# Audio tower on one core: TensorE's first four slots written out, and a norm on ScalarE

## The reference

```
p   = patches of 16 samples, stride 8                  # 64 x 32 tokens x 1024
h   = relu(p @ W1 + b1) @ W2 + b2                      # 64 x 32 tokens x 256
h  += attention(h)       # 16 heads, "bit-linear": input normalised, quantised to 127 steps,
                         # ternary weights wq, wk, wv; softmax; again normalised, quantised, wo
h  += gate * (norm(h) @ w_expert + b)                  # top-1 of 8, capacity 100 per expert
h  += real part of a decayed linear recurrence over norm(h)
h  += sum over the top 2 of 8 experts: (silu(n @ M1) * (n @ M2)) @ M3,  n = norm(h)
```

## Time and profile before

| | us |
|---|---|
| median of 3 runs | 538.47 (538.28 to 539.43) |
| profiled execution, its own time | 540.12 |
| profiled execution, span from the first to the last instruction | 538.1 |
| TensorE busy (matrix products) | 433.2, 81% |
| VectorE busy | 303.9, 56% |
| ScalarE busy | 199.4, 37% |
| GpSimd busy | 162.2, 30% |
| granted TensorE clock, mean | 0.91 of 2.4 GHz |

### The profile page before, as it was taken

One profiled execution on the slowest core, in us unless ns is written; L12 is line 12 of the kernel. 1 busy time (PEld: TensorE's weight loads), 2 busy tenths in 40 slices (PEclk: granted clock), 3 DMA queues, 4 the chain that ended last, 5 costly groups with the idle time before them and its releaser, 6 DMA issues.

```text
span 538.1 us, 9170 instructions
## 1 busy us (share of the span) xinstructions
PE 433.2 (81%) x3291; PEld 282.7 (53%) x3292; DVE 303.9 (56%) x869; ACT 199.4 (37%) x369; POOL 162.2 (30%) x140
## 2 busy tenths in 40 slices
PE   0698798888657754737759999999799999999991
PEld 0254455555554543536525766676565666566561
DVE  0596958784699899998897577726431111111110
ACT  0244545254357513113422662254323233223321
POOL 6041010010020023531042546353254343454422
PEclk9999998979977957855679999999999999999997
DMA  9999010072054100543010422243123226232311
GB/s 179 245 211 204 13 32 3 25 248 84 15 164 179 34 13 2 177 153 132 10 40 11 118 39 41 40 118 50 27 43 49 50 39 185 49 58 39 48 22 19
DMA packets 36102, 43.14 MB, mean 80 GB/s; under 512 B 5216, under 2 KB 30560, under 8 KB 35904
## 3 DMA queue, kind: packets, MB, share of 16 engines
q1 hardware_dynamic: 26384, 32.14, 21.5%
q0 software_dynamic: 7488, 10.23, 12.1%
q10 hardware_dynamic: 2192, 0.27, 0.5%
HBM read 30.96 MB, written 11.53 MB: 79 GB/s over the span
## 4 chain that ended last, share of the span: by engine, by line
PE 57%; DVE 23%; DMA 7%; issue 7%; ACT 3%; SPq 1%; POOL 0%; POOLq 0%; DVEq 0%; ACTq 0%
PE psum L2026 22%; PE psum L2045 11%; PE psum L1723 8%; DMA KT<-in_L_attn_w_o_dram 3%; PE psum L2036 3%; PE psum L1736 2%; PE psum L1748 2%; DMA out_dram<-mixture_rows_out 2%; PE psum L1761 2%; PE psum L2016 1%; DVE st_att L998 1%; DMA KT<-mixture_rows_in,src_i 1%; DVE mx L1032 1%; PE psum L1852 1%; DVE O L1194 1%
## 5 line engine op out<-in xcount | busy, mean ns | idle before, releaser
L1625 DVE TENSOR_TENSOR QT<-QT,psum 128x512 f32<-128x512 f32 x39 | 26.8, 688 | 134.6 <-PE psum L2026 134.4
L1723 PE MATMUL psum<-M2s,M1s 128*128 128x512 f32 x128 | 60.3, 627 | 21.3 <-DMA M1s<-in_L_tok_W_dram 18.8
L2026 PE MATMUL psum<-M1s,KT 128*128 x156 | 75.5, 607 | 1.4 <-ACT KT L789 1.0
L2045 PE MATMUL psum<-M3s,KT 128*128 x312 | 74.2, 381 | 1.5 <-ACT KT L797 0.8
L2026 PE MATMUL psum<-M2s,KT 128*128 x156 | 73.3, 592 | 0.0
L2045 PEld LDWEIGHTS psum<-M3s,KT 128*128 128x128 f32 x312 | 58.5, 190 | 22.0 <-issue 15.9
L808 ACT ACTIVATE O<-psum,gate_slot 128x256 f32<-128x256 f32 x39 | 18.5, 474 | 108.8 <-PE psum L2045 106.0
L502 POOL DMA_INDIRECT KT<-mixture_rows_in,src_i x39 | 41.0, 1052 | 44.2 <-issue 23.3
L1723 PEld LDWEIGHTS psum<-M2s,M1s 128*128 128x128 f32 x128 | 25.1, 201 | 50.6 <-issue 30.0
L2026 PEld LDWEIGHTS psum<-M2s,KT 128*128 128x128 f32 x156 | 29.8, 191 | 37.6 <-issue 37.6
L529 POOL DMA_INDIRECT mixture_rows_out<-O,src_i x17 | 31.6, 1860 | 31.3 <-ACT O L808 12.5
(11 more groups left out here) (398 smaller groups left out, 732.6 us busy)
## 6 DMA issues: line engine op xcount, KB each, us to landing
M3s<-in_x_dram SPq DMA_DIRECT2D x4, 1024.0 KB, 10.6
M3s<-in_L_ffn_W_dram SPq DMA_DIRECT2D x1, 4096.0 KB, 14.3
M2s<-in_L_ffn_W_dram SPq DMA_DIRECT2D x1, 4096.0 KB, 14.8
M1s<-in_L_ffn_W_dram SPq DMA_DIRECT2D x1, 4096.0 KB, 14.0
M3s<-in_x_dram SPq DMA_DIRECT2D x4, 992.0 KB, 14.5
M1s<-vtok SPq DMA_DIRECT2D x64, 34.0 KB, 1.9
mixture_rows_out<-H SPq DMA_DIRECT2D x4, 512.0 KB, 4.2
M1s<-in_L_tok_W_dram SPq DMA_DIRECT2D x2, 512.0 KB, 14.2
```

The source lines that it names most:

```text
L1625: v.tensor_tensor(sil[:, u, :], sil[:, u, :], bank[3], ALU.mult).then_inc(v_gated, 1)
L1723: last = mm(bank[6 + c], W1s[:, r, P * c:P * (c + 1)], xr[:, i % 2, r].rearrange("p b l -> p (b l)"), start=(n == 0), stop=(n == STRIDE - 1))
L2026: last = mm(z, xrT[:, u, c, :], w[:, bass.ds(e, 1), c, :].rearrange("p a h -> p (a h)"), start=(c == 0), stop=(c == CH - 1))
L2045: last = mm(bank[6][:, 0:DM], actT[:, u, c, :], M3s[:, bass.ds(e, 1), c, :].rearrange("p a d -> p (a d)"), start=(c == 0), stop=(c == HC - 1))
```

## The change

TensorE's queue for slots 0 to 3 is written out step by step, and the loop goes on from slot 4. `layer1` takes a range of the eight products, and small products stand between the parts. In slots 1 to 3 the second relu stands later on ScalarE, behind the copy of the transposed input; `embed` stands behind the twelve copies in slot 3 too; TensorE's second layer of step 2 stands between the two pairs of values, and so does that of step 3, which stood ahead of the output projection. The rounding of the attention's rows is done by ScalarE in all slots. The norm ahead of the first expert goes to ScalarE for steps 2 and 3 (`NORM2_ACT = 2`), and VectorE's `expert_added` is cut in two in the tail.

```diff
+        NORM2_ACT = 2
@@ ScalarE
+            def att_quant(i):
+                act.wait_ge(v_att_scale, i + 1)
+                for t in range(TS):
+                    r = a.activation(O[i % 2][:, t, :], O[i % 2][:, t, :], ACT.Copy, bias=MAGIC,
+                                     scale=SD["s"][:, t:t + 1])
+                r.then_inc(a_att_quant, 1)
+            def norm2_rows(i):
+                act.wait_ge(v_norm2, i + 1)
+                for t in range(TS):
+                    a.activation(O[i % 2][:, t, :], H[:, TS * i + t, :], ACT.Identity, bias=SD["am"][:, t:t + 1],
+                                 scale=SD["rstd"][:, t:t + 1]).then_inc(a_norm2, 1)
...
-                if iA is not None and iA > 0:
-                    hidden(1)
...
-                layer2_last = iB is not None and iD is None
-                if iA is not None and not layer2_last:
-                    embed(iA)
                 if iA == 0:
+                    embed(0)
...
                     a.activation(xqT[:].rearrange("p c n -> p (c n)"), bank[4].bitcast(BF16), ACT.Copy).then_inc(a_xqT, 1)
+                if iA is not None and iA > 0:
+                    hidden(1)
                 if iC is not None and iN is None:
                     exps(iC, range(2, BT))
...
-                if iA is not None and layer2_last:
+                if iA is not None and iA > 0:
                     embed(iA)
...
                     wait(act, v_xq_rows, done(slot, B_LAG))
+                    if iD >= NORM2_ACT:
+                        norm2_rows(iD)
                     norm2_columns(iD)
@@ ScalarE, tail
-            att_columns(STEPS - 1)
+            att_quant(STEPS - 1)
             act.wait_ge(p_values, BT * STEPS)
             norm(SR, 1, X4[1], v_norm4_in, a_norm4)
+            att_columns(STEPS - 1)
             norm4_columns(1)
             act.wait_ge(p_scores, BT * STEPS)
             norm(SE, 2, N3_of[2], v_norm3_in, a_norm3)
+            norm2_rows(STEPS - 1)
@@ VectorE
             def att_quant(i):
-                for t_ in range(TS):
-                    ln(v.tensor_scalar(Oi[:, t_, :], Oi[:, t_, :], SD["s"][:, t_:t_ + 1], MAGIC, ALU.mult, ALU.add))
-                own()
+                dve.wait_ge(a_att_quant, i + 1)
                 wait(dve, p_oqT, i)
...
             def att_norm2(i):
                 answered()
+                if i >= NORM2_ACT:
+                    minus_mean(SD, v_norm2)
+                    return
...
                 if iC is not None:
                     minus_max(iC, 0)
                     minus_max(iC, 1)
+                if iD is not None and not together:
+                    att_quant(iD)
@@ VectorE, tail
-            att_quant(last)
+            v.engine_nop().then_inc(v_att_scale, 1)
             answered()
             minus_mean(SR, v_norm4_in)
-            expert_added(2, bank[6])
+            expert_gate(2, bank[6])
+            att_quant(last)
+            expert_sum(2)
@@ TensorE
-                for n, r in enumerate(order):
+                for n, r in list(enumerate(order))[lo:hi]:
...
             def norm2_columns(i):
                 pe.wait_ge(v_norm2, i + 1)
+                wait(pe, a_norm2, TS * (i + 1 - NORM2_ACT))
...
+            layer1(1, 0, 0, 4)
+            batch_mean_in(0, 1)
+            layer1(1, 0, 4)
+            layer1(1, 1, 0, 3)
+            in_columns(0)
+            layer1(1, 1, 3)
+            qkv(0, 1)
+            layer2(1)
+
+            layer1(2, 0, 0, 3)
+            scores(0, 2, range(0, 2))
+            layer1(2, 0, 3, 6)
+            batch_mean_in(1, 2)
+            layer1(2, 0, 6)
+            scores(0, 2, range(2, BT))
+            layer1(2, 1, 0, 4)
+            in_columns(1)
+            layer1(2, 1, 4)
+            qkv(1, 2)
+            values(0, 2, range(0, 2))
+            layer2(2)
+            values(0, 2, range(2, BT))
+
+            layer1(3, 0, 0, 5)
+            pe.wait_ge(v_att_rows, 1)
+            att_mean(0)
+            layer1(3, 0, 5)
+            scores(1, 3, range(0, 2))
+            layer1(3, 1, 0, 2)
+            batch_mean_in(2, 3)
+            layer1(3, 1, 2, 5)
+            scores(1, 3, range(2, BT))
+            layer1(3, 1, 5, 7)
+            att_columns(0)
+            layer1(3, 1, 7)
+            in_columns(2)
+            pe.wait_ge(a_hidden, CH * STEPS)
+            att_proj(0)
+            qkv(2, 3)
+            values(1, 3, range(0, 2))
+            pe.wait_ge(v_att_added, 1)
+            layer2(3)
+            values(1, 3, range(2, BT))
+            wait(pe, v_less_max, BT * done(3, C_LAG))
+            norm2_columns(0)
+            pe.wait_ge(d_we, 48)
+            pe.wait_ge(a_embed, STEPS)
+            expert_rows(0)
+
+            for slot in range(STEPS, SLOTS_OF_STEPS):
```

More of the change, by code:

```diff
@@ L1855, in expert_rows, with batch_mean_in @@
                        ).then_inc(p_expert, 1)
[L1857 to L1865 removed]
+            def batch_mean_in(i, slot):
+                pe.wait_ge(v_batch_in, i + 1)
+                wait(pe, v_att_rows, done(slot - 1, C_LAG))
+                mm(bank[2][:, 0:TS], batch_mean[:], SB1["bs"][:, 0, :], start=True, stop=True).then_inc(p_batch_in, 1)
@@ new lines, in _ @@
+            layer1(0, 0)
+            pe.wait_ge(g_const, 19)
+            pe.wait_ge(v_abs_sum, 1)
+            mm(bank[2][:, 0:4], ones[:], wsum[:], start=True, stop=True).then_inc(p_abs_sum, 1)
+            layer1(0, 1)
+            layer2(0)
+            pe.wait_ge(v_ternary, 1)
+            for c in range(CH):
+                for w in range(4):
+                    for o in range(CH):
+                        last = tr(bank[4 + c].bitcast(BF16)[:, DM * w + P * o:DM * w + P * (o + 1)],
+                                  wter[:, w, o, P * c:P * (c + 1)], ident_b[:])
+                last.then_inc(p_ternaryT, 1)
@@ L1896, in _ @@
                 if iB is not None:
[L1897 to L1906 removed]
+                    in_columns(iB)
                 if iD is not None:
[L1908 removed]
                     wait(pe, a_expert, TS * done(slot - 1, D_LAG))
@@ L1912, in _ @@
                 if iB is not None:
[L1913 to L1926 removed]
+                    qkv(iB, slot)
                 if iC is not None:
```

115 lines of the change are left out of this document (41 added, 74 removed).

## The result

The changed kernel takes 532.82 us (median of 4 runs, 530.51 to 533.99), the kernel before 538.95 beside it (4 runs, 538.28 to 540.51). The medians differ by 6.1 us. The ratio is 0.9866, 95% interval 0.9843 to 0.9889, which stands for 7.2 us (6.0 to 8.5). The forecast was 11.9 us, and 526.6 us with a range to 531.5. Both are faster, and both fall short of 11.9 us: the first set lies outside the range, the second just inside it. The profiled execution took 533.95 us, its span is 532.2.

A forecast was written before the change was run, and what follows sets the result against it. Before the mixture, queue order bounds slot 3 and VectorE slot 4; TensorE is busy 245.07 of 262.20 us after. Terms 1.3 + 1.2 + 6.9 + 0.4 + 1.2 + 1.0 - 0.1 = 11.9 us give 526.6 us, range 523.8 to 531.5.

The forecast's parts named there:

- the largest term: Slot 3: cut products hide waits such as 2.16 us at the input's mean, and the clock stays up; gain 6.9 us.
- The 3.1 us of clock: Part of slot 3's 6.9 us: no fall to 1.2 GHz behind the wait at 110.14.
- Slot 1 and slot 2 up to the projections: Slot 1 hides TensorE's 1.25 us wait, gain 1.3; slot 2 runs without a wait up to its projections.
- slot 4's entry: VectorE's wait for the experts' gate rows shrinks, so slot 4 moves by 0.4 us more.
- both terms of slot 5: VectorE gives quantising passes to ScalarE, gain 1.2 us; its norm of step 2 goes there too, gain 1.0.
- signs of being wrong: Clock 0.50 between 85 and 117 us, gap before values over 2.5 us, or ScalarE's norms ending after TensorE is ready.
- Slot 4 has the same queues as before: Slot 4: nothing gained or lost inside it, 0 us.
- The second half as long as before: The mixture's slots, from 275.8 us on in the kernel before: length unchanged, 0 us.
- Slot 2's gain: The second layer covers the 1.57 us wait for VectorE's transposes; slot 3 starts at 98.2, 1.2 us more gained.
- the first rival: New waits before values in slots 2 and 3 bring 1.2 GHz; up to 3.1 us per fall, 529.7 to 532.8; chance 0.17.
- the case that no fall adds to it: The forecast itself, 526.6 us with its gain of 11.9 us; chance 0.67.
- The tail: Rounding rows come up to 1.3 us earlier, but step 3's norm queues on ScalarE; taken as 0.1 us loss.

The follow-up runs named there:

- e8_before_early: The kernel before with only the 4 MB load of M2s moved to slot 3, right behind that of M3s: 539.19 us, ratio 0.9985.
- e5_halves: The changed kernel with slot 3's two halves of layer 1 whole again, the second layer still behind the first values: 537.7 us, ratio 0.9965.
- c_after: The changed kernel run again as a second set with nothing altered: 530.65 us, ratio 0.983 to the kernel before.
- f1_norm_step2: The changed kernel with step 3's second norm back on VectorE and step 2's kept on ScalarE: 530.05 us, ratio 0.9817 to the kernel before.
- e2_m2early: The changed kernel with the 4 MB load of M2s moved to slot 3, right behind that of M3s: 529.07 us, ratio 0.9808 to the kernel before.
- e1_cover: The changed kernel with slot 2's second layer put back between projections and values: 531.37 us, ratio 0.9838 to the kernel before.
- e4_actpart: The kernel before with all edits but TensorE's order and the relu and embedding that go with it: 539.59 us, ratio 1.0001.

## Why the prediction was wrong

The direction was right. The mechanism of the largest term too: slot 3 gave 6.4 of 6.9, for the reasons named, with no fall of the clock inside the slot in any of 13 profiles, where all four with the halves whole have one behind the wait of 2.16 us, and with waits where they were forecast (1.69, then 0.7 and 0.3 in the projections, which I had counted in ScalarE's twelve copies). The 3.1 us of clock in it were sized by a profile with the longer fall; in e8_before_early and e5_halves the fall costs 1.7. Slot 1 and slot 2 up to the projections, slot 4's entry (0.2 for 0.4) and both terms of slot 5 (1.3 and 1.0 for 1.2 and 1.0) held. Of the signs of being wrong two came: a clock of 0.50 between 85 and 117 us, in the first profile and not in c_after, and in the tail norms on ScalarE that end after TensorE is ready for them (1.37 us at 252.61). These steps failed:

- **"Slot 4 has the same queues as before"**, cost 0, measured -1.3 in both profiles. The step moved against a load that SyncE issues when the values' copies are out, and the stall inside the scores went from 2.21 to 3.20 us. The stall stood in the timeline of before as an "issue" wait with a load beside it, and I left it out. That the load brings the stall is shown by moving it; that the change makes it longer is less sure, since it was 1.94 us in f1_norm_step2.
- **"The second half as long as before"**, cost 0, measured -2.3 and -1.2. The profile before had no fall of the clock at slot 17; eight of twelve have one. It costs 1.7 us in the first profile and in c_after (5.6 us for the two groups of products instead of 3.9); the other 0.6 of the first profile has no cause shown. A single execution was read as the rule.
- **Slot 2's gain** (1.2, and 1.3 of slot 1 with it) came nearly whole (2.2 to 2.5 us) in seven of nine profiles and was lost in the first. That is the first rival, in the place it named, with one fall at 2.5 us for its bound of 3.1; 529.7 to 532.8 as its time, 532.82 measured. That the time fits is in part luck: the rival had two falls in slots 2 and 3 for 532.8, and there was one, beside the stall and the mixture, which it did not have. It had 0.17, while the case that no fall adds to it had 0.67. The argument against it, that the wait of 1.69 us brought none, holds for that place (none in 16 profiles) and said nothing of slot 2; and I overlooked that in the same profile of the kernel before the clock is 0.50 from 86.7 us on in slot 2, behind a wait of 1.12 us. It costs nothing there, since slot 3 starts at 100.72, and at 100.56 and 100.79 in the two profiles of the old order without it. The row at 113.6 that the prediction leans on shows TensorE busy 3.40 of 3.40 us at the lower clock; it shows that the clock was low behind a wait, and not what ends it.
- **The tail** (-0.1) gave +0.6: both of its terms came as counted, 1.3 us earlier at the third norm's transposes for the rounding rows and 1.3 lost behind them for the norm (5.24 us before, 6.50 after; f1_norm_step2 has 5.24 again). What it had not counted is a clock that came back 1.1 us sooner in the expert rows, worth 0.5.
- **Terms were added as if none could be given back.** e2_m2early's 1.5 us at the tail's last transposes were 0.1 at the slot tables, by the clock of the expert rows. ScalarE's half, forecast at 2.1 us, had them at the slot tables of its profile and measured 0.0 in time.

The range doesn't follow from its terms either: 526.6 less 2 is 524.6, not 523.8, and 1.5 falls and the tail's 1.2 above it are 532.5, not 531.5. The two falls of the first rival, 532.8, lay outside it from the start.

What the first profile shows is then the 9.2 us of c_after less a fall in slot 2 (2.1) and 1.1 more lost in the mixture. How often the executions of a set fall can't be read from times alone, so the 3 us between the medians' gains in the two sets (2.0 by the ratios, whose intervals overlap) are not settled beyond this; the chips may differ too. Not settled either: why the instruction packet in slot 4 starts as late as it does, from 6.3 to 7.9 us behind the input's mean, with the same load beside it.

## What to carry to other kernels

Read the kernel before in more than one execution before its clock is taken as given: a wait of 1.1 to 2.3 us on TensorE had the fall behind it in some executions and not in others in slot 2 and in the mixture, in all of them at slot 3's input mean, and a forecast has to price it at its share. Cut large products to stand between small ones where their inputs come late (4.8 us here in one slot), fill what waits remain with work that is needed anyway, and keep large loads away from a place where TensorE shows an "issue" wait inside a run of products; the "instruction" rows of the DMA queues tell whether a packet comes late there. Where VectorE was full, a faster TensorE paid nothing, and a norm moved to ScalarE was paid back where TensorE waited for it.

## What the runs showed of the hardware

- Behind the mixture's wait of 2.1 to 2.3 us the products ran at 2.4 or at 1.2 GHz, by the execution: eight profiles of twelve fell. Behind 1.61 us in slot 2 two of ten did (e1_cover is the tenth). Behind the 2.16 us of slot 3's whole halves all four did, which cost 1.7 us in two (e5_halves, e8_before_early) and 3.2 in two (the kernel before, e4_actpart). Behind the 1.69 us ahead of slot 3's projection none of 16 did, and behind the 2.16 us there in e5_halves the one did.
- A 4 MB load at 402 GB/s beside TensorE's scores cost a stall of 3.2 us without a releaser; at 377 GB/s beside layer 1, the projections and the second layer it cost none.
- The packet of the instruction queue at that place takes 0.96 to 0.97 us with the load and 0.96 to 1.29 without, and starts 6.3 to 7.9 us behind the input's mean with it, 2.9 to 3.6 without.
- In the tail the clock came back 3.1 us (changed kernel) to 6 us (e2_m2early) behind the expert rows' first product: at 256.5 us where they started at 253.45, at 258 where they started at 251.99.
